# Tile 0's rows and the first part of W1T asked for ahead of the edge lists in a graph attention kernel

## What is computed

```python
n = (x - mean(x)) / sqrt(var(x) + 1e-5)          # per row
h = (n @ W1.T).reshape(1250, 8, 128)
a_src = einsum('nhc,hc->nh', h, att_src)         # and a_dst with att_dst
e = leaky_relu(a_src[src] + a_dst[dst], 0.2)
alpha = segment_softmax(e, dst)                  # over the edges of a destination
out = segment_sum(alpha * h[src], dst)           # then bias, relu, second layer, residual, FFN
```

## Time and profile before

| | |
|---|---|
| median of 3 runs | 733.01 us (731.76 to 735.08) |
| span of the profiled execution | 730.7 us |
| TensorE (PE) busy | 718.9 us, 98% of the span |
| VectorE busy | 518.6 us, 71% |
| ScalarE busy | 390.7 us, 53% |
| GpSimd busy | 112.2 us, 15% |
| DMA, mean over the span | 108 GB/s |
| DMA, 12 to 15 us | 416 GB/s |
| granted TensorE clock | highest tenth in each of the 40 slices |

### The profile page before, as it was taken

The page is one execution under the profiler, slowest core; times in us unless marked ns, Lnnn a source line. Parts: engine busy times, 40 slices in busy tenths (PEclk is TensorE's granted clock), DMA queues, the critical chain, the costliest instruction groups (busy, mean ns, idle before and its releaser), DMA issues.

```text
span 730.7 us, 13048 instructions
## 1 busy us (share of the span) xinstructions
PE 718.9 (98%) x4607; PEld 655.4 (90%) x4607; DVE 518.6 (71%) x940; ACT 390.7 (53%) x749; POOL 112.2 (15%) x95
## 2 busy tenths in 40 slices
PE   8899999999999999999999999999999999999998
PEld 6699999789899999999999999999999898978965
DVE  5899888699999999999999452336567543717141
ACT  4665574388698889888888931122231413322100
POOL 2569330000000000000000000000233330222211
PEclk9999999999999999999999999999999999999999
DMA  8627655759121221302230020001873544215011
GB/s 284 206 81 213 190 165 153 191 164 333 37 71 36 71 61 45 105 21 85 76 132 0 0 57 1 1 0 36 259 255 90 174 136 156 92 61 175 22 37 49
DMA packets 39665, 78.92 MB, mean 108 GB/s; under 512 B 4074, under 2 KB 25392, under 8 KB 38721
## 3 DMA queue, kind: packets, MB, share of 16 engines
q1 hardware_dynamic: 33932, 60.53, 27.2%
q10 hardware_dynamic: 4500, 13.82, 5.8%
q0 software_dynamic: 1184, 3.92, 1.8%
HBM read 62.97 MB, written 15.29 MB: 107 GB/s over the span
## 4 chain that ended last, share of the span: by engine, by line
PE 94%; DMA 3%; ACT 1%; DVE 1%; issue 0%; ACTq 0%; SPq 0%; POOL 0%; POOLq 0%; DVEq 0%
PE bank L1240 23%; PE bank L1382 15%; PE bank L1219 12%; PE bank L1311 12%; PE bank L1117 11%; PE bank L1458 5%; PE bank L1478 5%; DMA w1n_sb<-in_W 3%; PE bank L1034 3%; PE bank L1363 1%; PE bank L1256 1%; PE bank L1036 1%; PE bank L1430 1%; PE bank L1446 1%; PE bank L1049 1%; PE bank L1493 1%
## 5 line engine op out<-in xcount | busy, mean ns | idle before, releaser
L1240 PE MATMUL bank<-PT,h1s 125*128 125x250 f32 x800 | 175.8, 374 | 0.0
L1240 PEld LDWEIGHTS bank<-PT,h1s 125*128 125x128 f32 x800 | 148.5, 190 | 15.7
L1824 DVE SCALAR_TENSOR_TENSOR L<-asb,nadh 125x1250 f32<-125x1250 f32 x80 | 118.0, 1517 | 3.1 <-PE bank L1219 1.3
L828 ACT COPY PT<-bank 125x500 f32<-125x500 f32 x200 | 99.8, 596 | 37.8 <-PE bank L1219 37.8
L1832 DVE CUSTOM_DVE_ANT_0 L<-L,LC 125x1250 f32<-125x1250 f32 x80 | 113.4, 1455 | 0.0
L815 ACT ACTIVATE L<-L,nm 125x1250 f32<-125x1250 f32 x80 | 107.8, 1371 | 0.0
L1219 PEld LDWEIGHTS bank<-ident,L 125*125 125x125 f32 x800 | 93.3, 189 | 3.9 <-ACT L L815 1.5
L1219 PE MATMUL bank<-ident,L 125*125 125x125 f32 x800 | 94.6, 273 | 0.7 <-ACT L L815 0.7
L2005 DVE TENSOR_TENSOR x2f<-bank,x2f 125x384 f32<-125x384 f32 x20 | 10.3, 552 | 63.4 <-PE bank L1478 63.4
L1641 DVE TENSOR_TENSOR hotr<-iota,r 125x1500 f16<-125x1500 f16 x50 | 46.5, 931 | 8.0 <-PE bank L1036 4.4
L646 POOL MEMSET pick<- 128x90 f32 x1 | 0.2, 168 | 277.8 <-ACT hT L856 277.8
(11 more groups left out here) (247 smaller groups left out, 1238.9 us busy)
## 6 DMA issues: line engine op xcount, KB each, us to landing
asb<-src_logit_rows SPq DMA_DIRECT2D x7, 1250.0 KB, 5.9
atom_w<-in_atom_inT SPq DMA_DIRECT2D x5, 1152.0 KB, 11.3
atom_w<-in_atom_outT SPq DMA_DIRECT2D x5, 1152.0 KB, 9.6
log_count_scratch<-LCw SPq DMA_DIRECT2D x10, 546.9 KB
LC<-log_count_scratch SPq DMA_DIRECT2D x10, 546.9 KB
LCt<-log_count_scratch SPq DMA_DIRECT2D x10, 546.9 KB
h_scratch<-h1st ACTq DMA_DIRECT2D x10, 448.0 KB
h1s<-h_scratch SPq DMA_DIRECT2D x7, 560.0 KB
```

What stands on the lines that cost most here:

```text
L828: act.copy(PT[(k - lag) % 2][:, 2 * b:2 * b + 2, :], bank[turned_bank(first, k - lag, b)][0:NP, 0:2 * GW].rearrange("p (s n) -> p s n", s= ...
L1240: mm = pe.matmul(bank[2 + (k - lag) % 2][:, 0:GW], h1s[q][:, s, :], PT[(k - lag) % 2][:, s, :], start=(s == 0), stop=(s == NT - 1))
L1824: dve.scalar_tensor_tensor(L[r][:, :], asb[q][0:NP, 1, :], nadh[q][:, t:t + 1], asb[q][0:NP, 0, :], ALU.add, ALU.max).then_inc(stt_done, 1)
```

## The change

SyncE asks for tile 0's rows ahead of the destination lists. ScalarE asks for the first part of W1T ahead of the source list, for the other two parts right behind it, and then does the small activation; its wait for the edges is gone. On VectorE tile 0's statistics stand ahead of the wait for the edges. On TensorE tile 0 is turned ahead of the spans. There are 42 fillers instead of 46 (24, 6, 8 and 4), and they write bank 0 instead of bank 3, which the turn of tile 0 now uses ahead of some of them.

```diff
@@ SyncE
+            load_x(0)
             for a, b in ((0, 80), (80, NS)):
                 sp.dma_start(dsr[a:b, :], dst_rows[a:b, :]).then_inc(edges_in, 16)
             for a, b in ROWS:
                 sp.dma_start(dsti[a:b, :], dst_cols[a:b, :]).then_inc(edges_in, 16)
-            load_x(0)
@@ ScalarE
-            for a, b in ROWS:
-                act.dma_start(srci[a:b, :], src_cols[a:b, :]).then_inc(edges_in, 16)
-            act.wait_ge(consts_made, 4)
-            act.activation(rstd[:, NT - 1:NT], tiny[:, :], ACT.Ln, bias=tiny[:, 0:1], scale=2.0)
-            act.wait_ge(edges_in, 3 * TWO)
             for k in range(0, KD, 2):
                 act.dma_start(w1_sb[:, k:k + 2, 0:HC], W1T.rearrange("(k p) n -> p k n", p=128)[:, k:k + 2, :]
                               ).then_inc(w1_in[k // 2], 16)
+                if k == 0:
+                    for a, b in ROWS:
+                        act.dma_start(srci[a:b, :], src_cols[a:b, :]).then_inc(edges_in, 16)
+            act.wait_ge(consts_made, 4)
+            act.activation(rstd[:, NT - 1:NT], tiny[:, :], ACT.Ln, bias=tiny[:, 0:1], scale=2.0)
             act.dma_start(w1n_sb[:, :, :], W1.rearrange("(h c) d -> c h d", c=C)).then_inc(w1n_in, 16)
@@ TensorE
-                    pe.transpose(bank[3][:, 0:128], ident[:, :], ident[:, :])
+                    pe.transpose(bank[0][:, 0:128], ident[:, :], ident[:, :])
             def spans_turned():
-                pe.wait_ge(consts_made, 2)
-                keep_busy(26)
                 pe.wait_ge(span_step, 6)
...
+            pe.wait_ge(consts_made, 2)
+            keep_busy(24)
+            turn(0)
+            keep_busy(6)
             spans_turned()
-            keep_busy(12)
-            turn(0)
+            keep_busy(4)
             first_products()
@@ VectorE
             dve.memset(attz[:, :, :], 0.0).then_inc(attz_set, 1)
-
-
+            first_statistics()
             dve.wait_ge(edges_in, 3 * TWO)
...
             s.then_inc(span_step, 1)
-            first_statistics()
             dve.wait_ge(span_turned, 1)
```

## The result

Four runs of the changed kernel took 738.93 to 740.39 us, median 739.10, beside 732.39 for the kernel before (four runs, 731.76 to 735.08). The ratio is 1.0093, with a 95% interval of 1.0072 to 1.0114: slower by 0.9%, 6.7 us. The profiled execution has a span of 738.5 us instead of 730.7. The forecast was 735.5 us with a range of 732.0 to 738.0; the time lies 1.1 us above its upper end. The profiled execution is the slowest of the four (740.39 us, the others 738.93 to 739.15), so the profiles differ by 7.8 us where the medians differ by 6.7.

The account below looks back on a forecast made before the run. TensorE fills 94% of the chain; at the start VectorE's chain from the edges to wrow sets the time. With the edges at 8.8 us, 730.7 + 2.5 = 733.2, plus 2.3 from span to median: 735.5 us, range 732.0 to 738.0.

Parts of the forecast that it names:

- What bounds the start: VectorE's chain from the edges' landing to wrow, with 0.77 us of slack, overtakes TensorE's own path and sets the time.
- The landing of the edges, T: Time the last of six edge transfers lands, which VectorE's spans wait for: 4.04 us before, forecast 8.8 us.
- the rows' own landing: Tile 0's rows, first on SyncE's queue, were to land between 2.8 and 4.9 us, ahead of VectorE's statistics.
- The sum T - 6.29: TensorE's delay where it turns wrow (L1174), from VectorE's shifted chain: 2.5 us late with T = 8.8.
- T + 4.4: Start of TensorE's first products (L1143), after spans, turns and fillers: 13.2 us with T = 8.8, instead of 11.55.
- The cover of the one-hots: VectorE's one-hots stay ready before TensorE reaches them; their cover of over 3 us shrinks but is not used up.
- under the wait for the edges: On TensorE, tile 0's six transposes, turn and copy were to cost nothing there; 0.8 us if that cover were gone.
- some 1.4 us: TensorE's forecast wait for VectorE's wrow at L1174, after arriving at 35.0 us; it then goes on 2.5 us late.
- (c): TensorE's clock falls in new gaps ahead of the first products: 737.6 us for 12 products, 744.7 for 36; chance 0.07.
- (a): Both queues serve the edge rows promptly, T 4.3 to 6.3: delay -2.0 to 0, 731.0 to 733.0 us; chance 0.12.
- (d): Waits downstream on TensorE swallow the shift: 733.0 us; chance 0.03.
- (b): Edges land a turn or more later, T 10 to 11.7: +3.7 to +5.4 us, 736.7 to 738.4; chance 0.16.

Follow-up runs that it names:

- The delay alone: The kernel before with four cleared rows of 1080 elements added on VectorE ahead of w_lo, no DMA or order changed: 740.29 us, ratio 1.0103.
- the run with fillers: The changed kernel with 20 filler transposes in TensorE's wait ahead of the turn of wrow: median 736.14 us, ratio 1.0052.
- the run of the queues alone: The kernel before with only the DMA order of the changed kernel, VectorE's and TensorE's order kept: 737.07 us, ratio 1.0050.
- the engines' order alone: The kernel before with only the changed order on VectorE and TensorE, old DMA order and wait for the edges kept: 737.34 us, ratio 1.0059.
- last version: The changed kernel with source list first on ScalarE, W1T waiting only for tile 0's rows, 12 fillers ahead of wrow's turn: median 734.14 us, ratio 1.0032.
- source list first: The changed kernel with the source list ahead of W1T's first part again on ScalarE's queue: one run, 737.9 us.
- before, 9 fillers: The kernel before with 9 fillers on TensorE between tile 1's turn and the plan's loads: median 733.56 us, ratio 1.0022.
- before, 2.5 us on VectorE: The kernel before with two cleared rows of 1080 elements added on VectorE ahead of w_lo: 736.15 us, ratio 1.0054.

## Why the prediction was wrong, point by point

**What bounds the start** was right: VectorE's chain from the edges' landing to wrow, with 0.77 us of slack, ahead of TensorE's own path. The delay alone (1.0103) shows that this chain is enough for the whole loss.

**The landing of the edges, T**, was taken as 8.8 and measured as 9.7, inside the forecast's bounds of 6.8 to 10. Taking it from small loads in W1T's traffic rather than from the 2.08 us of empty queues was the right choice. What I named as the reason was partly wrong: less the 375 KB of rows ahead of them than W1T's traffic beside both makes what is on SyncE's queue late, and it hit the rows themselves. The rows ahead cost the edges 1.4 us without that traffic (5.5 instead of 4.0), and 5.7 with it. I had bounded the rows' own landing by 4.9 from the 4.1 us of before; they were read at 6.7. This bound was taken from a stretch in which W1T didn't flow, the same mistake that I avoided for the edges.

**The sum T - 6.29** held. With T = 9.71 it gives 3.4, and 3.35 was measured; with the 9.21 of the run with fillers it gives 2.9, measured 2.86. In the other kernels with this order of the engines it is right to 0.1 us too, if T is read as the start of the spans and what VectorE waits for the turned spans beyond 0.48 us is added. First products were forecast at T + 4.4 = 14.1 and came at 14.14; this was in part luck, for in the run with fillers, with TensorE at the low clock until 15 us, they came at 14.73 where T + 4.4 is 13.6. That TensorE's own lateness costs nothing was right too: in the run of the queues alone they came at 18.8 and the wait just shrank. The cover of the one-hots, said to be "not used up", was: TensorE waited for them twice, 0.19 us at 27.3 and 0.32 us at 28.6, which cost nothing as it had 2.50 us to wait at wrow anyway.

**The clock is the step that failed.** The prediction had TensorE wait "some 1.4 us" at L1174 and then went on with the sum as if nothing followed. The only rival on the clock, (c), placed its fall ahead of the first products, where it did fall (0.50 from 10.5 to 12 us) and cost nothing, as VectorE was later anyway. At L1174, where TensorE has the whole rest of the run behind it and no slack, it cost 4.4 us, more than the 3.35 of the delay. With it, and with the measured T, the sum would have been 730.7 + 3.4 + 4.4 = 738.5, the measured span. The late edges alone stay inside the range: 730.7 + 3.4 + 2.3 = 736.4.

**From span to median.** The prediction kept 2.3 us between the profiled span and the median. In the changed kernel it was 0.6 (739.1 against 738.5). That the forecast missed its range by only 1.1 us is partly due to this: with 2.3 us kept, the measured span would have meant 740.8.

**Rivals.** (a), edges early enough, and (d), absorbed downstream, fell. (b), later edges, didn't come about: T was below 10. (c) had the right mechanism, the clock, at the wrong place, and a small chance, 0.07. What neither held: the new order of the engines is harmful by itself (1.0059), which I had set down as costless "under the wait for the edges". If that cover were gone I had priced it at 0.8 us; it was 1.46 us of VectorE's waiting, behind statistics that had to wait for rows.

**What stays open.** Fillers in the wait removed the fall (changed kernel) or most of it (last version), and an added wait brought it. But in two profiles it fell after waits of 0.16 and 0.44 us at this place. And longer waits elsewhere brought no fall: 2.30 us ahead of the spans' turn (source list first) and 1.26 us ahead of L1169 (before, 9 fillers). The start of the fall also differs, from 0.3 us before TensorE took up wrow (changed kernel) to 3.3 us after it (before, 2.5 us on VectorE). So the wait isn't the only thing that counts; whether the thin products around it (16 columns wide in L1168 and L1151) count too was not tried.

## What to carry to other kernels

A step that waits only to keep a large transfer off the queues may look like a lost opportunity and be the thing that keeps small, urgent loads fast: before lifting it, look at what small loads took while the large one flowed. When two engines take turns, compute the slack of the later chain at each place where they meet, and if a sum leaves TensorE waiting over a microsecond where all that follows hangs on it, price the products behind the wait at half the clock too.

## What the runs showed of the hardware

The four loads of 3 and 4 KB that SyncE issued beside W1T's 1 MB parts took 6.7 to 10.6 us from issue to landing in the kernels that ask for W1T by 1.9 us, and 1.7 to 2.3 us in the three that have the rows first and W1T held back to 4.7 or 5.5 us. Tile 0's 375 KB of rows took 7.7 us behind the edge lists beside W1T, and 3.4 us from the last issue without W1T.

The granted clock of TensorE fell to 1.2 GHz for 3.4 to 10.2 us around and after the wait for wrow, mostly where that wait was 1.1 to 3.3 us, in a stretch of thin products; this cost 1.4 to 4.5 us. With 20 transposes of the identity in the wait it stayed at 2.4 GHz. The same fall in the first 15 us cost nothing in the changed kernel, where VectorE was later, and 0.8 us at wrow with the engines' order alone, where VectorE waited 1.46 us for the turned spans and not 0.48.
